# Attention cores of a four-layer program: four heads to a group, sums apart from the values, and another order of products

## What is computed

```python
# layer 0: 16 heads of 32; 496 keys, and 16 further keys with a softmax of their own
ctx = _attn(qT, k.transpose(0, 2, 1, 3), v.transpose(0, 2, 1, 3))
ctx_dca = _attn(qT, k_dca.transpose(0, 2, 1, 3), v_dca.transpose(0, 2, 1, 3))
ctx = ctx + DCA_WEIGHT * ctx_dca
...
# layer 3: 32 heads of 16, 512 keys, rotary positions on q and k
logits = jnp.einsum('bqhd,bkhd->bhqk', q, k) * scale
w = jax.nn.softmax(logits, axis=-1)
attn = jnp.einsum('bhqk,bkhd->bqhd', w, v)
```

## Time and profile before

| | us |
|---|---|
| median of 3 runs | 3682.25 (3680.83 to 3690.68) |
| profiled execution, its own time | 3679.52 |
| its span in the trace | 3677.7 |
| first core (228.6 to 607.5) | 378.9 |
| last core (2690.3 to 3136.6) | 446.3 |
| PE busy over the span | 2622.3 (71%) |
| DVE busy | 2358.2 (64%) |
| ACT busy | 1590.1 (43%) |
| POOL busy | 994.7 (27%) |

### The profile page before, as it was taken

The page is one execution under the profiler, slowest core; times in us unless marked ns, Lnnn a source line. Parts: engine busy times, 40 slices in busy tenths (PEclk is TensorE's granted clock), DMA queues, the critical chain, the costliest instruction groups (busy, mean ns, idle before and its releaser), DMA issues. The chain is left out here.

```text
span 3677.7 us, 45536 instructions
## 1 busy us (share of the span) xinstructions
PE 2622.3 (71%) x13916; PEld 1204.5 (33%) x13916; DVE 2358.2 (64%) x4171; ACT 1590.1 (43%) x2191; POOL 994.7 (27%) x874
## 2 busy tenths in 40 slices
PE   3978998799564375276667479972978888748991
PEld 1532333344231131021112257751522222324760
DVE  6656664555735535698889766656667777455664
ACT  3534543244221134444444245541646666222870
POOL 5760000000000112476667222215640000001434
PEclk9979999799676586598899689995979999859995
DMA  3542101110000000000000167753531100111995
GB/s 130 206 152 75 58 13 58 38 35 23 3 0 9 19 0 0 1 1 0 0 0 0 46 217 238 238 168 106 227 126 70 51 8 13 76 51 61 331 314 162
DMA packets 148632, 305.96 MB, mean 83 GB/s; under 512 B 18323, under 2 KB 65439, under 8 KB 146038
## 3 DMA queue, kind: packets, MB, share of 16 engines
q1 hardware_dynamic: 125542, 223.49, 17.2%
q0 software_dynamic: 22928, 80.49, 6.7%
HBM read 210.34 MB, written 93.32 MB: 83 GB/s over the span
## 5 line engine op out<-in xcount | busy, mean ns | idle before, releaser
L1970 DVE TENSOR_REDUCE ac_nmax<-ac_M 128x1 f32<-128x512 f32 (+1 forms) x768 | 496.4, 680 | 214.8 <-PE ac_M L1822 213.1
L1951 ACT ACTIVATE ac_PT<-ac_S 128x1024 f32<-128x1024 f32 x384 | 386.1, 1017 | 184.8 <-PE ac_S L1851 182.3
L2700 PE MATMUL sc_y<-sc_hc,ident 128*128 128x512 f32 x512 | 294.1, 659 | 140.9 <-POOL sc_hc L2676 140.5
L2676 POOL TENSOR_TENSOR sc_hc<-sc_h,sc_cs 128x512 f32<-128x512 f32 x256 | 324.2, 1267 | 174.1 <-DVE sc_h L2778 170.2
L2778 DVE TENSOR_TENSOR_SCAN sc_h<-sc_dA,sc_dB 128x512 f32<-128x512 f32 x256 | 309.9, 1212 | 9.7 <-ACT sc_dA L2738 9.7
L1867 PE MATMUL ac_o<-ac_PT,ac_V 128*32 128x512 f32 (+1 forms) x1536 | 276.9, 614 | 1.0 <-ACT ac_PT L1951 0.8
L2738 ACT ACTIVATE sc_dA<-sc_dl,sc_A 128x512 f32<-128x512 f32 x256 | 176.4, 690 | 177.3 <-DVE sc_h L2778 177.3
L2700 PEld LDWEIGHTS sc_y<-sc_hc,ident 128*128 128x128 f32 x512 | 79.6, 193 | 333.5 <-POOL sc_hc L2676 330.4
L2770 DVE TENSOR_TENSOR sc_dB<-ss_du,sc_b 128x512 f32<-128x512 f32 x256 | 168.5, 659 | 15.8 <-PE sc_b L2690 15.8
L1822 PE MATMUL ac_M<-KT,QT 64*128 64x512 f16 (+1 forms) x384 | 133.5, 421 | 41.8 <-DVE ac_nmax L1970 28.6
L813 POOL DMA_INDIRECT mo_g<-normalised,mo_cur x112 | 146.3, 1306 | 61.4 <-POOL mo_cur L809 44.3
(11 more groups left out here) (482 smaller groups left out, 5866.1 us busy)
## 6 DMA issues: line engine op xcount, KB each, us to landing
slot_results<-mo_o SPq DMA_DIRECT2D x56, 512.0 KB, 4.0
mo_up<-in_w_gate SPq DMA_DIRECT2D x24, 704.0 KB, 5.5
mo_up<-in_w_up SPq DMA_DIRECT2D x24, 704.0 KB, 6.9
keys_t<-ap_kto SPq DMA_DIRECT2D x32, 512.0 KB, 2.6
queries_t<-ap_qto SPq DMA_DIRECT2D x32, 512.0 KB, 2.7
mo_up<-in_exp_up SPq DMA_DIRECT2D x32, 512.0 KB, 6.4
mo_dn<-in_exp_down SPq DMA_DIRECT2D x32, 512.0 KB, 7.2
mo_dn<-in_w_down SPq DMA_DIRECT2D x24, 512.0 KB, 7.3
```

The source lines that it names most:

```text
L1951: nc.scalar.activation(PT[:, n % PTB, :, :], psS[:, 2 * (n % 2):2 * (n % 2) + 2, :], ACT.Exp, scale=SCALE / (SQK * SQK)).then_inc(exp_done, 1)
L1970: last = v.tensor_reduce(out[:, :, 0], sc[:, 0:MAIN], AX.X, ALU.max)
L2676: nc.gpsimd.tensor_tensor(hc[:, m % RC, :], h[:, m % RH, :], cs[:, n % 2, :], ALU.mult).then_inc(hc_done, 1)
L2700: nc.tensor.matmul(py[:, c, :], env.id32[:], hc[:, m % RC, :], start=(n == 0), stop=(n == NS - 1)).then_inc(y_mm, 1)
```

## The change

First core: a group has four heads with 32 columns each, and `V` and `Vd` are the plain loaded values without a column of ones (no memset, no spread, both batches' tiles loaded directly). The sums of exponentials come another way: GpSimd adds the exponentials of key blocks 0, 1 and 2 (`partial_sums`, into `psum3`), and TensorE multiplies these by a column of ones and the exponentials of block 3 by the two mask columns (`sums`: main keys and further keys). ScalarE copies that too (`sums_out`), it is turned first (`turned(g, 2)`), VectorE takes the reciprocals (`inverse`) and multiplies twice (`normed`); the addition of the two softmaxes goes to GpSimd (`combine`). `PT` has six tiles instead of three, freed by values and by sums or additions (`slot_free`). A step is now two units in both cores.

Last core: a step's order on TensorE becomes two maxima, four scores (two units), two maxima, values, and then rows or output transposes where they are due.

Both: `QT` is laid out [partition, head column, 512], so its loads are four DMAs (one for each query block) with 256-byte pieces on the side of `QT`; the rows of maxima of a group go in two DMAs instead of four or eight; maxima run 34 ahead (before: 18 in the first core, 38 in the last); rows are turned eight units before they are needed.

```diff
-    VC = 1024 // H
-    GH = P // VC
-    NG, NP = H // GH, GH // 2
...
-    PTB = 2 * NP if rope else 3
-    UPG = TPB * NP
-    NMG = GH * TPB
-    TG, TU, TM = B * NG, B * NG * UPG, B * NG * NMG
-    EARLY = 2 if rope else 0
-    AHEAD = 2 * NMG + 2 + 2 * EARLY
+    PTB = 4 if rope else 6
+    UPG, NMG = TPB * NP, GH * TPB
     UB = NG * UPG
+    TG, TU, TM = B * NG, B * UB, B * NG * NMG
+    LEAD = 8
+    AHEAD = NMG + 2 + 2 * LEAD
...
+        at_rows = {g * UPG - LEAD: g for g in range(1, TG)}
...
+                    sp.dma_start(QT[b % 2][row:row + 1, c:c + NR // 2, :],
+                                 mrow[i * NR // 2:(i + 1) * NR // 2, g % 2:g % 2 + 1, :]).then_inc(row_in[g % 2], 16)
...
-                for buf, src in ((KT, "kt_d"), (QT, "qt_d")):
-                    g.dma_start(buf[b % 2][:], w[src][b * TPB:(b + 1) * TPB].rearrange("j p (c q) -> p j c q", q=P)
+                g.dma_start(KT[b % 2][:], w["kt_d"][b * TPB:(b + 1) * TPB].rearrange("j p (c q) -> p j c q", q=P)
+                            ).then_inc(kq_in[b % 2], 16)
+                for j in range(TPB):
+                    g.dma_start(QT[b % 2][:, :, j * P:(j + 1) * P], w["qt_d"][b * TPB + j].rearrange("p (c q) -> p c q", q=P)
                                 ).then_inc(kq_in[b % 2], 16)
...
+            def partial_sums(G, kt):
+                for p in range(NP):
+                    n = G * UPG + kt * NP + p
+                    pool.wait_ge(exp_done, n + 1)
+                    if kt == 1:
+                        if G:
+                            pool.wait_ge(sum_mm, G)
+                        first = PT[:, (n - NP) % PTB]
+                    else:
+                        pool.wait_ge(p_added, G * 2 * NP + p + 1)
+                        first = psum3[:, p]
+                    g.tensor_tensor(psum3[:, p], first, PT[:, n % PTB], ALU.add).then_inc(p_added, 1)
+            def combine(G):
+                pool.wait_ge(b_done, G + 1)
+                c0 = G % NG * GH * HD
+                av = A[:, :, c0:c0 + GH * HD].rearrange("p j (h d) -> p j h d", d=HD)
+                g.tensor_tensor(av, av, tmp[:], ALU.add).then_inc(a_sum, 1)
...
+                output_weights()
+                for b in range(2, B):
+                    pool.wait_ge(sT_done, (b - 1) * UB)
+                    load(b)
+                    spread(b)
+                    if b + 1 < B:
+                        load_values(b + 1)
+            else:
+                load_values(1)
+                g.memset(ones[:], 0.0)
+                ch.link(g.memset(which[:], 0.0))
+                g.memset(ones[:, 0:1], 1.0)
+                ch.link(g.tensor_copy(which[:, 0:2], w["mask"][:]))
+                g.sem_inc(const_done, 1)
+                output_weights()
+                for G in range(TG):
+                    b = G // NG
+                    if G % NG == 0 and b and b + 1 < B:
+                        pool.wait_ge(sT_done, b * UB)
+                        pool.wait_ge(pv_done, b * UB)
+                        load(b + 1)
+                        load_values(b + 1)
+                    partial_sums(G, 1)
+                    partial_sums(G, 2)
+                    if G:
+                        combine(G - 1)
+                combine(TG - 1)
...
+            def sums(g):
+                if g == 0:
+                    pe.wait_ge(const_done, 1)
+                pe.wait_ge(d_ev, g + 1)
+                pe.wait_ge(p_added, (g + 1) * 2 * NP)
+                for r in range(GH):
+                    nc.tensor.matmul(px[r * VC:(r + 1) * VC, :], ones[:], psum3[:, r // 2, r % 2, :], start=True, stop=False)
+                for r in range(GH):
+                    n = g * UPG + (TPB - 1) * NP + r // 2
+                    last = nc.tensor.matmul(px[r * VC:(r + 1) * VC, :], which[:], PT[:, n % PTB, r % 2, :], start=False,
+                                            stop=True)
+                last.then_inc(sum_mm, 1)
...
+            scores_t(1)
+            for n in range(0, TU, 2):
+                g, s = n // UPG, n % UPG // 2
+                if rope:
                     more(n)
+                scores_t(n + 2)
+                scores_t(n + 3)
+                if g and s == 3 and not rope:
+                    turned(g - 1, 1)
+                if rope:
+                    more(n + 1)
+                    values(n + 1)
+                else:
+                    more(n)
                     values(n + 1)
                     more(n + 1)
+                if n in at_rows:
+                    maxima_rows(at_rows[n])
+                if g and rope and s == 2:
+                    turned(g - 1, 0)
+                if g and not rope:
+                    if s == 0:
+                        sums(g - 1)
+                    elif s < 3:
+                        turned(g - 1, 2 if s == 1 else 0)
+            if rope:
+                turned(TG - 1, 0)
             else:
+                sums(TG - 1)
+                for i in (2, 0, 1):
+                    turned(TG - 1, i)
...
+            def slot_free(n):
+                g, kt, p = of_unit(n)
+                act.wait_ge(pv_done, n - p + NP)
+                if rope:
+                    return
+                if kt == TPB - 1:
+                    act.wait_ge(sum_mm, g + 1)
+                else:
+                    act.wait_ge(p_added, g * 2 * NP + (kt == 2) * NP + p + 1)
...
+                if u == 1 and g:
                     group_out(g - 1)
+                if u == 3 and g and not rope:
+                    sums_out(g - 1)
+                if n - 3 in at_rows:
+                    group_rows(at_rows[n - 3])
...
+            for n in range(0, TU, 2):
+                g, s = n // UPG, n % UPG // 2
+                if g and s == 3 and not rope:
+                    normed(g - 1, 1)
+                for k in (n, n + 1):
+                    for m in maxima_of(k):
+                        maximum(m)
+                if g and s == 2:
+                    normed(g - 1, 0)
+                if g and s == 1 and not rope:
+                    inverse(g - 1)
```

281 lines of the change are left out of this document (135 added, 146 removed).

## The result

The changed kernel takes 3649.12 us (median of 4 runs, 3643.32 to 3651.56) against 3681.54 us for the kernel before on the same chip (3680.81 to 3690.68): ratio 0.990, 95% interval [0.988, 0.992]. Its profiled execution took 3648.04 us, span 3646.3. I forecast 3636 in a range of 3604 to 3666: the sign of every large term and the size of most held, and the time came out 13 us above the forecast, inside the range.

The account below looks back on a forecast made before the run. The first core was taken as bound by TensorE's issue, the last by a TensorE-VectorE loop over maxima banks. First core -55, last core +3 and query tile +5 us from 3679.5 gave 3632.5, stated as 3636 by the median, range 3604 to 3666.

Parts of the forecast that it names:

- Group of four heads in the first core: First core: four heads take 18.05 us against 21.72 before, as 32-column value products cost 1.0 a step instead of 2.0.
- Startup hole: First core's start: GpSimd scales output weights before its first addition, stalling the first sums by 14.6 us, between 5 and 20.
- no stall: First core: lower end of its term, -65 us, against a forecast of -55 and an upper end of -37.
- so nothing: Both cores: eight or four row transfers a group become two; no steady-state wait hangs on them, so no gain.
- hidden up to about 4 us each: First core: GpSimd's additions of 128x1024 lie hidden; above about 4 us each they would be the bound.
- Query tile: Loads in 256-byte pieces take 10.8 us instead of 5.9, delaying projection stores: +5 us, 0 to +20.
- Last core: New step order: step 3.08 instead of 3.30 us, but exposed transposes make a group 13.4 against 13.28: +3 us, -5 to +15.
- gains in full: Rival, last core: VectorE's output work finds another gap, group 12.5 us, -24 instead of +3, total 3609; chance 0.13.
- Sum: Whole kernel: 3679.5 - 55 + 3 + 5 = 3632.5 us, by the median 3635, stated as 3636.
- query loads hold GpSimd: Rival: issuing query loads takes GpSimd 14 us each, delaying additions; slower than before, 3683 or 3751 at longer issues; chance 0.06.

Follow-up runs that it names:

- Taking the weights away: Changed kernel, but GpSimd scales the first core's output weights behind the additions of groups 1 to 4 instead of before its first addition: 3629.3 us.
- the kernel with rows apart: Changed kernel with its new query tile, but one transfer per row, eight a group in the first core and four in the last: 3670.0 us.
- the kernel with the old tile: Changed kernel with the query tile laid out as before (4 KB pieces) and eight or four row transfers a group: 3631.7 us.
- clearing in pieces: Changed kernel, but GpSimd clears each value tile of the last core in eight pieces of 128x512 instead of one of 128x4096: 3646.9 us.

## Why the prediction was right, and where it was off

- **Group of four heads in the first core: right.** 17.90 for 18.05, the four steps with it, value products at 1.0. Ten steady groups gave 1.5 us more than forecast.
- **Startup hole: mechanism right, size 6 us short.** I put the first sums 58.4 us after the core's start; they came at 64.1. 3.1 of it is the first piece of the weights, landed 24.5 after the start instead of 21.4: it stands behind 5.25 MB of loads, of which the query tile's 2 MB move at 216 GB/s. I had costed these small pieces and not carried them to this wait. The other 2.6 lie behind the hole of 13.6 us; 1.8 of them are two rows of value products at the lower clock (1.94 and 1.92 us instead of 1.06 and 1.04), a cost that I left out of every stall. Taking the weights away gave 17 us in the first core and 20 in the median. One sum of mine is off: I called the lower end, -65, "no stall", but without the stall of 14.6 the same sum gives -70; -65 is a stall of 5.
- **Row transfers "so nothing": wrong at two places.** No steady group waits, as I said; but at each batch change the transfer queues behind the loads, 2.6 and 2.1 us of wait and 5.4 of longer groups. And the merging whose price I put at nothing is worth 21 us beside the small pieces, as the kernel with rows apart shows.
- **Additions "hidden up to about 4 us each": wrong, at no cost here.** My working had exponential 7 come 4.7 us after the sums "just then": the margin was zero. I then gave the limit from the sum of work. Measured: 0.2 us of margin, groups grow from 3.6 us each, and one more tile hides them again.
- **Query tile: right in kind, half the size, and by another path.** +5 forecast for both projections; layer 0's took 6.0 us more up to the core's start, layer 3's 3.0 (5.2 against the kernel with the old tile). The rate was forecast at 195 GB/s and is 216 to 221. I had counted the longer transfer only. What I missed is SyncE: it issues the four loads for 13.1 us instead of 1.9 and 0.7, and the stores behind them wait for that. I had put this cost on GpSimd, as a rival, where it did not come. A third place was missing too, the last core, by way of GpSimd's clearing. The Trainium skill, "DMA: Bandwidth & Descriptors", section Specifications, wants 512 bytes or more in a transfer for line rate; the trace agrees, with 216 to 221 against 358 GB/s.
- **Last core: right.** +3.7 for +3, step 3.08 for 3.08, group 13.43 for 13.4. Its opposite, the rival "gains in full" (-24), was not what the kernel did, but is what it does once the transposes lie under VectorE's maxima: 449.6 to 425.2. One thing I had not seen is inside the 3.7: 3.2 us are VectorE held by GpSimd's clearing, which clearing in pieces took away. Without them the core would be at +0.5, so that the total hit +3 is in part luck.
- **Sum.** By the profile the gain is 15.6 us below my sum: first core 8.6 (5.7 hole, 5.4 batch changes, less 1.5 of groups and a rest of 1.0), projections 4.0, last core 0.7, less 1.4 behind it, and 3.7 more between the cores. These 3.7 us lie between the first core's last store and layer 3's projection, in unchanged code (1945.4 us before, 1949.1 now). In the profiled executions of all fourteen kernels, which share this code, the stretch is 1943.3 to 1950.5 us long, with no pattern by edit: 3.7 us are within that scatter, and no cause in the change is shown.

The rival "query loads hold GpSimd" did not come: four transfers take it 4.6 us to issue, not the 14 that the count of pieces gave, and no steady addition waits for them. On SyncE's queue the four took 13.1.

## What to carry to other kernels

Work of a helper engine stays hidden up to two limits, its sum of work and the first deadline inside it; the second is found by asking which buffer is reused next, and here it was 0.2 us away while the sum had 7 us to spare. A layout that makes one transfer cheaper must be costed at everything that stands behind the dearer one: transfers, and instructions of the engine that issues it. A reordering must be costed at the round trip that it uncovers: put the round's parts under the neighbour's work, and the gain that was given back (24 us here) comes. And a one-off on a helper engine's queue, like the scaling of weights, belongs behind the first work that others wait for.

## What the runs showed of the hardware

- **VectorE held by GpSimd.** A VectorE scaling of 128x16 or 128x32 from SBUF to SBUF, 0.165 us in the median, took 4.26, 2.67 and 3.83 us and ended each time with a pass of GpSimd (clearing, copy, additions), while maxima read from PSUM beside the additions of a steady group kept their 0.67 us. The kernel before has one such hold too, 2.26 us at 242.32. The Trainium skill, "SBUF — State Buffer", section "SBUF: two separate sides", says that the two engines share a pair of ports under an exclusive lock and the later one fully blocks; the trace agrees in that VectorE is blocked and not slowed, but not in the rest. A hold can outlast one instruction: at 341.55 GpSimd was in an addition, the next addition and a third pass followed, and the scaling ended with the third, although a fourth began at 345.28. And in the first two holds the scaling had come 0.7 us before the clearing or the copy began, while GpSimd was issuing a transfer. What ends a hold is not shown.
- **Pieces of 256 bytes** moved 216 and 221 GB/s at a full share and above, from GpSimd's queue and from SyncE's alike, large ones 358.
- **The clock behind a hole.** In and behind 13.6 us without a product TensorE's granted clock was 0.50 (280 to 290), then 0.62 up to 295 and 1.00 from there, and eight value products took 1.94 us instead of 1.06. After a row wait of 6.0 us (rows apart) the scores took 1.89 instead of 1.04. A stall costs more than its own length.
- **Issuing.** GpSimd took 0.77 us for the query tile's 2 MB in large pieces (before) and 4.62 for the four transfers of 512 KB in small ones. SyncE took 0.70 and 1.93 us for the former, 13.06 and 13.08 for the latter.
